# Cross-attention in a three-layer decoder kernel: the context handed over with features as rows, so that the kernel no longer turns it

## What is computed

```
def _L0_xattn_ref(x, y, Wq, bq, Wkv, bkv, Wo, bo):     # y: the context, 8 x 1601 x 96
    q = x @ Wq + bq
    kv = y @ Wkv + bkv
    k, v = jnp.split(kv, 2, axis=-1)                    # 16 heads of 8 features
    attn = jnp.einsum('bhqd,bhkd->bhqk', q, k) * scale
    attn = jax.nn.softmax(attn, axis=-1)
    out = jnp.einsum('bhqk,bhkd->bhqd', attn, v)
    return out.transpose(0, 2, 1, 3).reshape(B, SQ, D_EMBED) @ Wo + bo
x = x + _L0_xattn_ref(_layernorm(x, axis=-1), ctx_768, ...)
```

## Time and profile before

| | |
|---|---|
| median of 3 runs | 1773.41 us |
| the three runs | 1774.05, 1773.41, 1769.02 us |
| profiled execution, its own time | 1769.51 us |
| its span, first to last instruction | 1767.5 us |
| mean granted clock of TensorE | 0.937 |
| PE busy over the span | 1551.0 us (88%) |
| DVE, ACT, POOL busy | 1113.3 us (63%), 931.6 us (53%), 555.9 us (31%) |

### The profile page before, as it was taken

The page is one execution under the profiler, slowest core; times in us unless marked ns, Lnnn a source line. Parts: engine busy times, 40 slices in busy tenths (PEclk is TensorE's granted clock), DMA queues, the critical chain, the costliest instruction groups (busy, mean ns, idle before and its releaser), DMA issues. The chain is left out here.

```text
span 1767.5 us, 29904 instructions
## 1 busy us (share of the span) xinstructions
PE 1551.0 (88%) x11045; PEld 847.0 (48%) x11045; DVE 1113.3 (63%) x2537; ACT 931.6 (53%) x2028; POOL 555.9 (31%) x690
## 2 busy tenths in 40 slices
PE   1677686699999999999999997899999997599999
PEld 1344343244454444454545443566666675244444
DVE  4755442477878686878787783566566654355554
ACT  1323233176777777776777676355555554243343
POOL 4010101121121203030303000688788885133331
PEclk9978787599999999999999999999999999699998
DMA  4222210703233323223132220000000000000001
GB/s 101 70 55 55 55 37 18 141 16 98 48 98 48 99 48 99 48 88 57 70 56 62 61 33 6 4 1 1 1 1 1 1 1 1 10 20 20 22 19 37
DMA packets 88422, 75.35 MB, mean 43 GB/s; under 512 B 24725, under 2 KB 78389, under 8 KB 87349
## 3 DMA queue, kind: packets, MB, share of 16 engines
q1 hardware_dynamic: 88276, 73.44, 18.9%
HBM read 42.73 MB, written 30.42 MB: 41 GB/s over the span
## 5 line engine op out<-in xcount | busy, mean ns | idle before, releaser
L1145 DVE TENSOR_REDUCE b_chunk_max<-psum 128x1 f32<-128x400 f32 (+1 forms) x1024 | 540.9, 569 | 176.7 <-PE psum L1359 170.6
L1283 ACT ACTIVATE b_prob<-psum 128x512 f32<-128x512 f32 (+1 forms) x832 | 451.2, 594 | 180.7 <-PE psum L1398 178.9
L1359 PE MATMUL psum<-k_stack,q_stack 128*128 128x400 bf16 (+1 forms) x1024 | 285.4, 343 | 21.0 <-DMA k_stack<-b_k_scratch 17.9
L1368 PE MATMUL psum<-b_prob,b_v_aug 128*32 128x256 f32 (+1 forms) x3328 | 265.9, 391 | 1.7 <-ACT b_prob L1283 0.4
L1398 PE MATMUL psum<-q_stack,k_stack 128*128 128x256 bf16 (+1 forms) x1664 | 253.0, 275 | 0.4 <-DMA q_stack<-b_mparts 0.4
L1398 PEld LDWEIGHTS psum<-q_stack,k_stack 128*128 128x128 bf16 (+1 forms) x1664 | 146.3, 99 | 117.9 <-ACT b_prob L1283 68.8
L1557 POOL TENSOR_SCALAR c_prob<-c_prob,c_rec 128x128 f32<-128x128 f32 (+1 forms) x256 | 191.9, 767 | 8.9 <-POOL c_kT L1566 8.3
L2036 DVE TENSOR_TENSOR e_hg<-e_gl,e_gate 128x512 f32<-128x512 f32 x128 | 123.3, 979 | 113.2 <-PE psum L2051 75.5
L1640 DVE SCALAR_TENSOR_TENSOR c_turned<-psum,c_bias,c_tab 128x256 f32<-128x256 f32 x256 | 106.1, 476 | 112.0 <-PE psum L1773 112.0
L1675 ACT ACTIVATE c_prob<-psum,c_mneg 128x128 f32<-128x128 f32 (+1 forms) x256 | 104.1, 419 | 136.7 <-DVE c_mneg L1617 136.7
L1359 PEld LDWEIGHTS psum<-k_stack,q_stack 128*128 128x128 bf16 x1024 | 99.7, 98 | 128.6 <-DVE b_chunk_max L1145 95.5
(11 more groups left out here) (213 smaller groups left out, 1971.0 us busy)
## 6 DMA issues: line engine op xcount, KB each, us to landing
k_stack<-b_k_scratch SPq DMA_DIRECT2D x32, 600.4 KB, 10.5
b_k_scratch<-b_kparts SPq DMA_DIRECT2D x7, 1200.8 KB, 4.4
b_k_scratch<-b_kparts SPq DMA_DIRECT2D x7, 800.5 KB, 6.3
b_ctx<-in_ctx SPq DMA_DIRECT2D x8, 576.0 KB
e_w<-in_L_ffn_re_w SPq DMA_DIRECT2D x62, 64.0 KB, 1.8
a_scratch<-a_parts SPq DMA_DIRECT2D x16, 192.0 KB, 2.2
k_stack<-a_scratch SPq DMA_DIRECT2D x16, 192.0 KB, 4.7
q_stack<-b_q_scratch SPq DMA_DIRECT2D x32, 96.0 KB, 2.2
```

Source lines behind the costliest of these rows:

```text
L1145: nc.vector.tensor_reduce(out=chunk_max[:, half, q, column4(hh), c:c + 1], in_=max_bank(v)[:, 0:w], axis=AX.X, op=ALU.max).then_inc(max_do ...
L1283: nc.scalar.activation(prob[0:k, buf, par * 2 * T:(par + 1) * 2 * T], st_bank(v, par)[0:k, :], ACT.Exp, scale=HD ** -0.5).then_inc(exp_don ...
L1359: nc.tensor.matmul(max_bank(T_.now("unit"))[:, 0:hi - lo], queries_of(qst, h, slice(q * P, q * P + P)), keys_of(kst, h, slice(lo, hi)), st ...
L1368: last = nc.tensor.matmul(pv[32 * hh:32 * hh + 32, :], v_aug[0:k, kt, g * GH + hh, :], prob[0:k, buf, c:c + T], start=(kt == 0), stop=(kt ...
```

## The change

`kernel()` transposes `ctx_768` to 96 x 1601 for each batch before it hands the array to the chip. One DMA then loads a batch straight into `b_ctxT`. The buffer `b_ctx`, the four "ctx" items with their transposes and copies, and their places in the tables go. Each "k" item moves one step ahead, to (0, 0), (0, 3), (0, 5) and (0, 7). `ctx_used` is raised behind ("v", 3) in place of ("ctx", 3). The three maxima banks and three score banks stay.

```
-PREP_AT = {(0, 0): ("ctx", 0), (0, 1): ("k", 0), (0, 2): ("pv", 0), (0, 3): ("ctx", 1), (0, 4): ("k", 1),
-           (0, 5): ("ctx", 2), (0, 6): ("k", 2), (0, 7): ("ctx", 3), (0, 8): ("k", 3), (0, 9): ("m", 2),
+PREP_AT = {(0, 0): ("k", 0), (0, 2): ("pv", 0), (0, 3): ("k", 1), (0, 5): ("k", 2), (0, 7): ("k", 3), (0, 9): ("m", 2),
            (0, 10): ("x", 0), (0, 11): ("q", 0), (0, 12): ("v", 0), (1, 0): ("v", 1), (1, 1): ("v", 2),
...
-PROLOGUE_ITEMS = [("ctx", 0), ("k", 0), ("ctx", 1), ("x", 0), ("q", 0), ("k", 1), ("ctx", 2), ("k", 2), ("ctx", 3), ("k", 3),
+PROLOGUE_ITEMS = [("k", 0), ("x", 0), ("q", 0), ("k", 1), ("k", 2), ("k", 3),
                   ("v", 0), ("v", 1), ("v", 2), ("v", 3), ("m", 0)]
...
-        sp.dma_start(self.ctx_sb[:, 0:KT - 1, :], src[0:(KT - 1) * P].rearrange("(k p) d -> p k d", p=P)).then_inc(self.ctx_loaded, 16)
-        sp.dma_start(self.ctx_sb[0:tile_rows(KT - 1), KT - 1, :], src[(KT - 1) * P:SKV]).then_inc(self.ctx_loaded, 16)
+        sp.dma_start(self.ctxT[:], src).then_inc(self.ctx_loaded, 16)
...
-                if kind == "ctx":
-                    cols = min(4 * P, SKV - 4 * P * g)
-                    nc.scalar.activation(ctxT[:, 4 * P * g:4 * P * g + cols], prep[0:DC, 0:cols], ACT.Copy).then_inc(prep_free, 1)
...
-                if kind == "ctx":
+                if kind == "k":
                     if g == 0:
-                        pe.wait_ge(ctx_loaded, T_.up("ctx", 32))
-                    for j, kt in enumerate(range(4 * g, min(4 * g + 4, KT))):
-                        k = tile_rows(kt)
-                        last = nc.tensor.transpose(prep[0:DC, j * P:j * P + k], ctx_sb[0:k, kt, :], ident[0:k, 0:k])
-                    last.then_inc(prep_full, 1)
-                    if g == 3:
-                        pe.wait_ge(prep_full, n)
-                        pe.sem_inc(ctx_used, 1)
-                elif kind == "k":
+                        pe.wait_ge(ctx_loaded, T_.up("ctx", 16))
                     lo, hi = CHUNKS[g]
                     nc.tensor.matmul(prep[:, 0:hi - lo], wkv[:, 0:D], ctxT[:, lo:hi], start=True, stop=True).then_inc(prep_full, 1)
...
                     last.then_inc(prep_full, 1)
+                    if g == 3:
+                        pe.wait_ge(prep_full, n)
+                        pe.sem_inc(ctx_used, 1)
...
-        v = _np.ascontiguousarray(inputs[name])
+        v = _np.asarray(inputs[name])
+        v = _np.ascontiguousarray(v.transpose(0, 2, 1) if name == "ctx_768" else v)
```

More of the change, by code:

```diff
@@ L831 @@
            (3, 2): ("pv", 3), (3, 4): ("attnT", 0), (3, 6): ("out", 0), (3, 9): ("m", 1)}
-NEXT_BATCH = ("ctx", "k", "x", "q", "v")
+NEXT_BATCH = ("k", "x", "q", "v")
 def prep_item(r, n, first=False, last=False):
@@ L867, in __init__ @@
         self.rows = sb("b_rows", [P, 2, D])
-        self.ctx_sb = sb("b_ctx", [P, KT, DC])
+        self.ctxT = sb("b_ctxT", [DC, SKV])
         self.w_loaded, self.ctx_loaded = sem("b_w_loaded"), sem("b_ctx_loaded")
@@ L900, in sem @@
             return ctx.enter_context(nc.semaphore(name))
-        wq, wo, wkv, bq, bk, rows, ctx_sb = pre.wq, pre.wo, pre.wkv, pre.bq, pre.bk, pre.rows, pre.ctx_sb
+        wq, wo, wkv, bq, bk, rows, ctxT = pre.wq, pre.wo, pre.wkv, pre.bq, pre.bk, pre.rows, pre.ctxT
         resid = sb("b_resid", [P, QT, D])
@@ L906, in cross_attention @@
         qparts = sb("b_qparts", [P, 3, T], BF16)
-        ctxT = sb("b_ctxT", [DC, SKV])
         kf, krest = sb("b_kf", [P, 2, CW]), sb("b_krest", [P, 2, CW])
@@ L950, in cross_attention @@
         PER = dict(item=len(PREP_AT), step=4 * KT, unit=4 * UNITS_B, group=4, batch=1, kchunk=4, half=2,
-                   stacked=8 * 16, m_stacked=4 * 64, dma=BOUNCES * 16, kdma=BOUNCES * 16, ctx=32, own_dve=NORM_LINKS + G + 2,
+                   stacked=8 * 16, m_stacked=4 * 64, dma=BOUNCES * 16, kdma=BOUNCES * 16, ctx=16, own_dve=NORM_LINKS + G + 2,
                    own_pool=4 * 2 + 2, mneg=4, vchunk=4, placed=2, out=1)
@@ L975, in load_ctx @@
                 sp.sem_inc(passed, 1)
[L976 removed]
+                src = a["ctx_768"][b] if isinstance(b, int) else a["ctx_768"][bass.ds(b, 1)].rearrange("a d s -> (a d) s")
                 pre.load_ctx(sp, src)
@@ L1190, in prologue @@
                 nc.vector.memset(v_aug[:], 1.0).then_inc(ones_set, 1)
-                T_.up("item", 14)
+                T_.up("item", 10)
                 for u in range(UNITS_B):
```

## The result

| | before | changed |
|---|---|---|
| median | 1771.21 us (8 runs) | 1763.65 us (8 runs) |
| lowest, highest | 1769.02, 1774.05 | 1757.66, 1766.96 |
| profiled execution (span) | 1769.51 (1767.5) | 1764.87 (1763.0) |
| PE busy | 1551.0 | 1537.7 |
| DMA packets | 88422 | 76276 |

The ratio is 0.995, with a 95% interval of 0.9937 to 0.9964, which is 6.4 to 11.2 us; the medians differ by 7.6 us. Forecast was a gain of 22 us, 1749, with 1742 to 1758 as range. The sign was right, the size was three times too large, and the measured median lies above the range.

A forecast was written before the change was run, and what follows sets the result against it. TensorE was taken as the bound, busy 448.64 of 464 us. Gains of 10.0 (PE items less drain), 7.0 (`k_stack` wait) and 5.2 (prologue) sum to 22.2 us, giving 1749 us, range 1742 to 1758.

The forecast's parts named there:

- part 1, PE's items in r = 0: Cross-attention loop: dropping three large ctx transpose groups and a small one saves PE 1.60 us a batch, over seven batches.
- part 1, drain at (1, 3): PE's wait for its own matmuls before raising ctx_used moves to ("v", 3) and stays a cost, 0.17 us a batch.
- part 2: Loop waits of PE for `k_stack` at (1, 9), 7.9 us, shrink by 7.0 us; bounds 3.5 and 7.9.
- part 3: Prologue: three ctx groups no longer hold up the k items; 5.2 us gained, bounds 4.0 and 6.0.
- part 4: Context load, now one DMA of 96 rows, is covered by 21.8 us before its first reader; booked at nothing.
- I book the two as equal: 0: ("k", 0) loses its 0.37 us copy wait; exponentials of (0, 1) behind two evacuations lose 0.2; booked at zero.
- the 0.47 stays: ("k", 1) takes the place of ("ctx", 1) behind ("pv", 0), so its 0.47 us wait for VectorE's `prep` remains.
- SyncE issues the k bounce at 589.27, when the last quarter is split: End of r = 0: the k parts' write to DRAM was taken to be issued at the last quarter's split.
- The k bounce starts one plain step earlier against that wait: With ("k", 3) a step earlier, the write of k parts to DRAM starts 1.45 us earlier against PE's wait at (1, 9).
- rival 1: Only PE work pays: q bounce holds the loads, or VectorE and ScalarE fill freed slots; 15.9 us, about 1755; 20%.
- rival 4: Context load arrives late if its rows go to one of 16 DMA engines; slower, 1809 us; chance 2%.
- what was said to show the prediction wrong: Scores waiting for ScalarE in (0, 1) and (0, 2), `k_stack` loads no earlier against PE, or first k item awaiting a DMA.

The follow-up runs named there:

- Experiment 2: Changed kernel with the k items back at (0, 1), (0, 4), (0, 6) and (0, 8), ctx items still gone: 1750.93 us, ratio 0.9896.
- experiment 1: Changed kernel with VectorE's norm_scale one step earlier, at (0, 1) instead of (0, 2): 1756.84 us, ratio 0.9925.
- experiment 3: Kernel before with norm_scale one step later, at (0, 3), where GpSimd splits the first quarter: 1768.81 us, ratio 0.9997.
- experiments 4 and 6: k parts written to DRAM by quarters, three ahead of the m stores: first on Experiment 2's kernel, 1744.02 us; second on the kernel before, 1761.58 us.
- experiment 5: Kernel without ctx items, with late k items and quarter-wise k writes; ctx_used now raised by ScalarE instead of PE: 1743.19 us, ratio 0.9844.

## Why the prediction was right in sign and wrong in size

The terms of the sum, with what each measured (loop terms for seven batches):

| term | forecast | measured |
|---|---|---|
| part 1, PE's items in r = 0 | 11.2 (7 x 1.60) | 3.6 |
| part 1, drain at (1, 3) | -1.2 (7 x 0.17) | -1.5 |
| part 2, wait for `k_stack` | 7.0 | 2.0 |
| part 3, prologue | 5.2 | 4.65 |
| part 4, context load | 0 | 0 |
| sum | 22.2 | 8.8 (medians: 7.6) |

Part 1's 3.6 is what came after the losses that the moved items brought; the price of the transposes itself was right.

**Part 1, the price of the transposes: right.** Experiment 2 takes them out and moves nothing else, and nine steps fall by 2.04 us: the forecast 1.60 and the 0.47 that ("ctx", 1) had to wait for ("pv", 0) would be 2.07, so the items' own price is 1.57. The Trainium skill's rule that the prediction weighed (TensorE: Matmul & The Clock Gate, "Back-to-back issue gap") would have given 1.05, by the prediction's estimate. Here the row was the better guide.

**Part 1, what the moved items meet: wrong, and the largest miss.** The forecast sum of the nine steps was 18.91 - 1.60 = 17.31 us, and it came to 18.39, 1.08 more: 7.6 us for seven. Two things make that up, less a gain, and a third stood as forecast.

- The step "I book the two as equal: 0" failed. The lateness of the exponentials cost 0.64 us in step (0, 2) (1.85 to 2.49), where the booking had 0.58 less 0.2 of overlap. The scores do wait. The gain of 0.37 did come, as 0.39, but with ("k", 0) moving out of step (0, 1); the copy's going alone gave none of it, since the wait for VectorE's maximum took its place (experiment 2). The net loss is 0.25 us a batch, a little beyond the bound of 0.2 and 1.8 us for seven.
- What the prediction left out: `norm_scale` on VectorE against GpSimd's split of quarter 0, 0.75 us a batch (experiment 1), 5.3 us for seven. It stood at nothing without a reason. The order of each engine's stream had been read, but not which instructions of two engines would now run at one time. Edits of PE's table move GpSimd's work as well, by way of ScalarE.
- The wait of which I said "the 0.47 stays" did stay (0.52 in experiment 1).

Together: 0.64 + 0.75 - 0.39 = 1.00 of the 1.08. The rest is 0.05 of the wait for ("pv", 0), 0.52 in place of 0.47, and 0.03 of the price, 1.57 in place of 1.60.

On such pairs the Trainium skill has a rule that speaks against this change and that the prediction did not weigh (SBUF — State Buffer, "SBUF: two separate sides"): VectorE and GpSimd share one pair of SBUF ports as an exclusive lock. VectorE's instruction takes it in a 2-port mode, or with two SBUF inputs against a GpSimd instruction that reads SBUF; whoever starts first holds it for the whole instruction, and the other waits. The runs agree in sign: 0.34 us alone, 0.87 to 1.20 beside a split. They agree in form: all 14 long ones in the changed kernel and all 7 in experiment 3 end 0.08 us behind the GpSimd instruction beside them. One seems to speak against it, since the record at 563.29 begins 0.07 ahead of GpSimd's (563.36) and is the longest, 1.20. But the first of the pair ends only at 563.37, and in the kernel before, too, the second record of a pair begins 0.08 before the first ends (569.40 and 569.48), so a record's start does not say who was first here. That a lock is the cause is the page's statement. The runs show that overlap and length go together: in the changed kernel and in experiment 3 the instruction is longer, in the cross-attention of the kernel before and of experiments 1 and 2, where it runs alone, it is not.

The prediction could have seen it in the kernel before. There the same line runs in the rotary attention too, and six of its 16 instructions take 0.88 us, each beside a GpSimd instruction of 0.72 (L1566). Six others, at 0.33, overlap only the last 0.25 us of such an instruction.

```profile
L127 DVE TENSOR_SCALAR xn<-x_sb,mv,rstd x16: 324/342/883, 1102.1 to 1396.1; 128x128 f32<-128x128 f32 x16
```

```profile
1206.78 0.88 DVE L127 TENSOR_SCALAR xn<-x_sb,mv,rstd 128x128 f32<-128x128 f32 x1
1206.85 0.72 POOL L1566 TENSOR_TENSOR c_kT<-c_turned 128x256 f32<-128x256 f32 x1
```

**Part 2: the premise failed.** "SyncE issues the k bounce at 589.27, when the last quarter is split" was not what held it. The earlier trace rows begin with the k bounce; one row further up stand the four issues of the m stores, 2.36 us long, which end at 589.15. The last split had ended at 588.00. "The k bounce starts one plain step earlier against that wait" was therefore false: when the split came earlier, SyncE was not free earlier, and the 1.45 us went into the distance from split to bounce (1.27 to 2.72). The loads did hang on the q bounce, as rival 1 has it: they follow its landing, in every batch. What shortened that landing was less to be written ahead of it: in experiments 4 and 6, with three quarters written earlier, the wait is gone with late k items, and in the kernel before. Of the 2.0 us that did come, a part is the drain at (1, 3), which brings PE to (1, 9) up to 0.22 us later in each batch that waits. The rest can't be laid to the change. The last q write lands 13.6 to 13.9 us behind the start of (0, 9) in some batches and 14.7 to 15.3 in others, in both kernels, and the long waits are those of the second group. Beyond the 2.03 of the step, PE takes 6.5 us before, 4.5 in the changed kernel, 3.9 in its second profile, 5.2 in experiment 2 with late k items, and 5.2 in experiment 3, which has the item table of the kernel before. Why the landing differs from batch to batch is open.

**Part 3: right, 4.65 for 5.2.** The loads were issued 321.89 - 316.12 = 5.8 us earlier, in a stretch that itself began 1.06 earlier. From the last split to the loads it took 5.68 us and not 4.68. The prediction had named some tenths for the quarters' DMAs coming closer together; they were a whole microsecond, if that is the reason, which no run isolates.

**Part 4: right.** No item waits for the context load, and rival 4 with its one engine fell. The load took 11.9 us, more than the 4.1 of its nearest row and the 2.7 at full rate, and in the batch shown it landed at 549.46, 9.9 us ahead of the first k item (559.37). The issues of the new load: KB, and us to landing.

```profile
b_ctxT<-in_ctx SPq DMA_DIRECT2D x8, 600.4 KB, 11.9
```

**The drain: right**, 0.22 for 0.17, and experiment 5 gave it back.

**The rivals and the range.** Of what was said to show the prediction wrong, two of three came: waits of the scores for ScalarE (in one of the two steps named), and `k_stack` loads no earlier against PE. Rival 1 came nearest, with 15.9 us at its floor and 12 beyond it, and 20%: it named VectorE, ScalarE and the norm's work in r = 0, and the q bounce, but neither the slowing of VectorE beside GpSimd nor the stores ahead of the k bounce. The floor was still too high, because each term's lower bound was set as if its own step held. Its evidence against, VectorE's free fifth, was an average: in the step in question VectorE had three maxima and the pv item queued.

## What to carry to other kernels

When a step moves, write down what each engine that reads its result will now run, and beside which instruction of which other engine, above all VectorE beside GpSimd. A mean busy share says nothing on a single step. For a DMA that is to go earlier, read the issuing engine's rows ahead of it: what stands last before the issue holds it, and what is still being written when it is issued sets when it lands. And an item that only frees time can be left at its old place first: here removing the ctx items alone gained 19 us, and removing them and moving the k items 8 to 10.

## What was unexpected of the hardware

- One TENSOR_SCALAR of 128x128 fp32 took 0.34 us by itself and 0.87 to 1.20 us beside GpSimd's TENSOR_TENSOR of 128x400, and ended 0.08 us behind it each time. GpSimd's own instructions kept their 0.95, 1.04 and 0.92 us on average.
- Between executions of one program the granted clock fell at different moments behind the rotary attention, and the 32 matmuls there took 3.84 or 6.79 us. The stretch behind the rotary attention was some 5 us longer where the clock fell early, two thirds of the gain that was measured.
